# Last stage of a convolution, attention and expert kernel: next image's divisions moved ahead of seven weighings, GpSimd's residual ahead of folds, router logits read in PSUM

## The reference, cut to what matters

```python
t = t + _L1_attn_ref(_ln_t(t), ...)          # softmax(q k) v + x, added to t
z = _ln_t(t)                                 # zero mean, unit variance per token
router_probs = softmax(z @ router_w + router_b)      # 8 experts
top_p, top_i = top_k(router_probs, 2)
top_p = top_p / sum(top_p)
expert_out = einsum('bnd,edc->bnec', z, expert_w) + expert_b
t = t + sum over the two chosen experts of top_p * expert_out
```

## Time and profile before

| what | value |
|---|---|
| time before, median of 3 runs | 2733.99 us (2731.76 to 2734.71) |
| the profiled execution's own time | 2732.48 us |
| its span in the profile | 2730.6 us |
| its mean granted clock of TensorE | 0.917 of full speed |
| PE busy | 2417.7 us (89%) |
| DVE busy | 2352.5 us (86%) |
| ACT busy | 1599.9 us (59%) |
| POOL busy | 394.4 us (14%) |

### The profile page before, as it was taken

How to read it: one execution, slowest core, us unless ns; L and a number is a source line. 1 busy time by engine, 2 the same in 40 slices (tenths; PEclk the granted TensorE clock), 3 DMA queues, 4 the chain that set the end, 5 groups by cost and what they waited for, 6 DMA issues and landing times. The chain is left out here.

```text
span 2730.6 us, 46984 instructions
## 1 busy us (share of the span) xinstructions
PE 2417.7 (89%) x18454; PEld 968.7 (35%) x18454; DVE 2352.5 (86%) x4150; ACT 1599.9 (59%) x2106; POOL 394.4 (14%) x456
## 2 busy tenths in 40 slices
PE   3878879269999999999999999999999998888886
PEld 1343334112222222222222222222222225767764
DVE  4577776599999999999999999999999973999997
ACT  1243343337777777777777777777777773333333
POOL 0011111300000001000000000000000001555555
PEclk9989999579999999999999999999999996766677
DMA  7686784420202212202202112022020002232321
GB/s 172 159 246 202 215 249 128 152 57 1 60 1 60 60 66 60 60 1 60 57 4 60 39 22 60 16 45 60 1 60 25 1 25 83 72 98 81 108 72 24
DMA packets 68110, 206.29 MB, mean 76 GB/s; under 512 B 20630, under 2 KB 33554, under 8 KB 61234
## 3 DMA queue, kind: packets, MB, share of 16 engines
q1 hardware_dynamic: 64034, 185.27, 24.3%
q0 software_dynamic: 3040, 15.57, 1.5%
q10 hardware_dynamic: 816, 2.46, 0.3%
HBM read 80.14 MB, written 61.31 MB: 52 GB/s over the span
## 5 line engine op out<-in xcount | busy, mean ns | idle before, releaser
L1331 DVE TENSOR_REDUCE at_XM<-at_psX 128x1 f32<-128x448 f32 x2688 | 1546.1, 619 | 88.6 <-PE at_psX L1182 67.9
L1248 ACT ACTIVATE at_PR<-at_psS 128x896 f32<-128x896 f32 x1344 | 1162.9, 915 | 451.2 <-PE at_psS L1158 449.1
L1200 PE MATMUL at_psV<-at_PR,at_V 128*32 128x448 f32 x5376 | 644.4, 551 | 0.1
L1158 PE MATMUL at_psS<-at_US,at_KS 128*128 128x448 f16 x2688 | 635.0, 356 | 0.6 <-ACT at_PR L1248 0.2
L1182 PE MATMUL at_psX<-at_KS,at_US 64*128 64x448 f16 x1344 | 489.7, 364 | 65.5 <-DVE at_XM L1331 43.0
L1182 PE MATMUL at_psX<-at_KS,at_UH 64*128 64x448 f16 x1344 | 489.7, 364 | 0.0
L1182 PEld LDWEIGHTS at_psX<-at_KS,at_US 64*128 64x128 f16 x1344 | 124.6, 93 | 720.0 <-DVE at_XM L1331 659.9
L1158 PEld LDWEIGHTS at_psS<-at_US,at_KS 128*128 128x128 f16 x2688 | 200.7, 98 | 272.7 <-ACT at_PR L1248 119.3
L1297 POOL CAST at_mrow<-at_mt 7x128 f16<-7x128 f32 x64 | 17.9, 279 | 1609.7 <-DVE at_mt L1350 1256.8
L1594 POOL TENSOR_TENSOR fi_WE<-fi_WE 128x256 f32<-128x256 f32 (+1 forms) x224 | 199.4, 922 | 197.0 <-DVE fi_WE L1647 197.0
L389 PE MATMUL psA<-sb_stacks,sb_lhs 128*32 128x448 f32 x1568 | 157.0, 547 | 0.8 <-DVE sb_X L841 0.8
(11 more groups left out here) (200 smaller groups left out, 2062.1 us busy)
## 6 DMA issues: line engine op xcount, KB each, us to landing
sums<-at_O SPq DMA_DIRECT2D x16, 1568.0 KB, 6.3
fi_SUMS<-sums SPq DMA_DIRECT2D x16, 1568.0 KB, 6.7
sb_stacks<-sb_T SPq DMA_DIRECT2D x64, 270.5 KB, 6.7
sb_stacks<-sb_Xp SPq DMA_DIRECT2D x64, 248.8 KB, 8.6
sb_stacks<-sb_Xp SPq DMA_DIRECT2D x64, 248.0 KB, 5.5
sb_stacks<-sb_T SPq DMA_DIRECT2D x64, 172.5 KB, 9.0
at_KS<-key_stacks SPq DMA_DIRECT2D x32, 208.0 KB, 6.8
fi_RES<-residual SPq DMA_DIRECT2D x16, 400.0 KB, 7.3
```

Source lines behind the costliest of these rows:

```text
L1158: last = nc.tensor.matmul(psS[:, at % 2, k, 0:TILE], KS[:, b, (2 * c + k) * P:(2 * c + k + 1) * P], US[:, b, t * TILE:(t + 1) * TILE], sta ...
L1200: last = nc.tensor.matmul(psV[C * q:C * q + C, 0:TILE], V[:, b, G * k + q, :], PR[:, (n * 2 * STEPS + 2 * q4 + q // 2) % PRS, q % 2, :], s ...
L1248: nc.scalar.activation(PR[:, f % PRS], psS[:, at % 2, :, 0:TILE], ACT.Exp).then_inc(p_ready, 1)
L1331: nc.vector.tensor_reduce(o, psX[:, (at + j) % 3, 0:TILE], AX.X, ALU.max).then_inc(x_done, 1)
```

## The change

In `finish`:

- VectorE does the inversions and divisions of image n + 1 directly behind L1696 and ahead of weighings 7 to 12.
- GpSimd does the residual of image n + 1 ahead of the folds that stand at s = 3 (the first fold of set 3, the second of set 2), and not behind all folds. In step 0, which has no folds, it stays where it was. Step 15 has no next image and so no residual.
- ScalarE's copy of the logits is gone. VectorE's L1707, L1708 and L1713 read them in PSUM; L1713 writes `LG` and gives `lg_ready`, for which TensorE's fifth set of sums waits.

```diff
@@ ScalarE
-                    act.wait_ge(l_full, n + 1)
-                    nc.scalar.activation(LG[:].rearrange("p k e -> p (k e)"), psL, ACT.Copy).then_inc(lg_ready, 1)
                     act.wait_ge(gap_ready, n + 1)
@@ GpSimd
+                nxt = n + 1 < N
                 if n > 0:
                     for s in range(QSETS + 1):
+                        if nxt and s == 3:
+                            residual(n + 1, (c + 1) % TURN, r + b)
                         if s < QSETS:
...
-                if n + 1 < N:
+                elif nxt:
                     residual(n + 1, (c + 1) % TURN, r + b)
@@ VectorE
                 nc.vector.tensor_copy(Z16[:, :, 3, :], Z16[:, :, 1, :]).then_inc(z16_ready, 1)
-                weigh(m, mb, range(7, NU))
                 if nxt:
                     invert(n + 1, 0)
                     invert(n + 1, 1)
                     settled()
                     for h in range(2):
                         divide(n + 1, (c + 1) % TURN, h)
-
-                dve.wait_ge(lg_ready, n + 1)
+                weigh(m, mb, range(7, NU))
+
+                dve.wait_ge(l_full, n + 1)
                 rev3 = rev[:].unsqueeze(1).broadcast_to([P, NC, E])
-                link(nc.vector.tensor_reduce(top1[:], LG[:], AX.X, ALU.max))
-                link(nc.vector.tensor_tensor(CAND[:], LG[:], per_token(top1[:], E), ALU.is_equal))
+                logits = psL.rearrange("p (k e) -> p k e", e=E)
+                link(nc.vector.tensor_reduce(top1[:], logits, AX.X, ALU.max))
+                link(nc.vector.tensor_tensor(CAND[:], logits, per_token(top1[:], E), ALU.is_equal))
...
-                link(nc.vector.scalar_tensor_tensor(out=LG[:], in0=SEL1[:], scalar=-3e38, in1=LG[:], op0=ALU.mult,
-                                                    op1=ALU.add))
+                nc.vector.scalar_tensor_tensor(out=LG[:], in0=SEL1[:], scalar=-3e38, in1=logits, op0=ALU.mult,
+                                               op1=ALU.add).then_inc(lg_ready, 1)
+                dve.wait_ge(lg_ready, n + 1)
```

## The result

| | before | after |
|---|---|---|
| median of 20 runs | 2733.35 us (2727.85 to 2738.29) | 2737.44 us (2730.19 to 2741.46) |
| profiled execution, its span | 2732.48, 2730.6 | 2734.93, 2733.1 |
| DVE busy | 2352.5 us | 2334.6 us |
| ACT busy | 1599.9 us | 1594.7 us |

The ratio is 1.0014, 95% interval 1.0007 to 1.0020: slower by 4 us, within the 0.2% that the forecast called no change. VectorE is busy for 18 us less, and the kernel is not faster.

What follows compares the result with a forecast made beforehand. VectorE bounds the kernel; its path changes by +0.75 + 0.01 - 1.73 + 0.45 = -0.52 us a step, but late clock rises hold steps at 27.3. +3.7 on 2734.0 gives 2737.7 us; case range 2733 to 2742, 8 in 10 2724.5 to 2745.

Steps and rivals of the forecast that it cites:

- The case it rested on: Last stage: short and long steps alternate with early and late clock rises, mean 27.3 us; chance 0.52.
- Part 1: Divisions ahead of weighings 7 to 12: TensorE's unit-9 experts and the work queued behind them come 1.11 us later.
- The break: Gap of 0.9 us in TensorE's burst after its first eight transposes, which can only delay the clock's rise.
- Part 2: Logits read in PSUM: L1707 begins 0.04 us behind the router; three reads cost 0.00 to 0.05 us a step.
- The Trainium skill's fixed cost: VectorE's three PSUM reads: 62 extra cycles each, 3.1 us in sum over 16 images; as a rival, chance 0.05.
- Part 3: Residual ahead of the folds: new stalls in VectorE's routing of 0.3 to 0.65 us a step, taken as 0.45.
- TensorE next: Experts of unit 2, slack 0.3 us: a late clock rise stalls VectorE's third weighing 1.2 to 1.8, taken as 1.45.
- The mean near 27.3: Steps of the last stage: mean length held at the spacing of the clock's rises, 27.3 us.
- the alternation that was drawn: Last stage: steps of about 26.5 and 28 us, short and long in turn.
- The ends: Step 0 gains 0.35 us, step 15 gains 0.45, where the alternation stands is worth up to 1; 0.7 taken off.
- the correction to the median: Profiled execution lay 1.5 us below the median, so +4.5 for it became +3.7 against the median of 2734.0.

Runs made afterwards that it cites:

- res_last: The changed kernel with GpSimd's residual put back behind all folds; 2736.70 us, ratio 1.0012 to the kernel before.
- fill: The changed kernel with eight transposes repeated in TensorE's wait for weighing 7; 2723.51 us, ratio 0.9965 to the kernel before.
- strewn: The changed kernel with inversions and divisions spread among weighings 7 to 12 and the residual two sets of folds later; 2717.35 us, ratio 0.9948 to before.
- psum_only: The kernel before with only the logits read in PSUM and ScalarE's copy gone; 2729.10 us, ratio 0.9982.

## Why the prediction was right

The forecast was +3.7 us on the median and the result +4.1. The case it rested on is the one that came: VectorE's saving is kept in steps with an early rise and taken back by a stall behind TensorE where the rise is late. That the number agrees within 0.4 us is in part luck, as the last three points say.

- **Part 1.** The break is 0.88 us (forecast 0.9), and the experts of unit 9 begin 1.91 us behind the first transpose where they began 0.83 behind it: 1.08 later, forecast 1.11.
- **Part 2.** Routing begins 0.04 behind the router, and the reads from PSUM cost 5 ns, nothing and nothing (groups of 16: 368, 367 and 362 ns long; from SBUF 363 for the reduce and 367 for L1713 of the kernel before). The Trainium skill's fixed cost ("VectorE: DVE Perf Modes", The TRN2 errata), 3.1 us by the estimate, does not appear.
- **Part 3.** L1711 to L1721 lose 0.23 to 0.26, 0.01, 0.02 and 0 or 0.17: 0.3 to 0.45, forecast 0.45. A step without a stall is 26.44 to 26.46, forecast 26.5. The rule that an operation with both inputs in SBUF waits for GpSimd's running instruction, read from two rows, held in all ten kernels: each such operation of 200 elements that met one ended at least 0.22 us behind it, most of them 0.22 to 0.23, and those that read PSUM did not wait. The Trainium skill has it as a lock ("SBUF — State Buffer", Who interferes with whom).
- **TensorE next.** The stall ahead of the third weighing is 0.95 to 1.52 us in eight steps, 1.22 in the mean (forecast 1.2 to 1.8, taken as 1.45), long steps are 27.4 to 27.9 (forecast 27.95). Late rises come 2.8 to 3.6 us behind the experts, forecast 3.0 to 4.5.
- **The mean near 27.3, and the reason given for it.** From step 3 to step 13 it is 27.40. The pattern is one short step to two or three long ones, and not the alternation that was drawn; that came in `res_last`. The reason, that the rises keep a spacing of 27.3 and hold the steps to it, is too simple. The rises of the changed kernel lie at 2384.4, 2411.7, 2439.0 and 2462.9, so 27.3, 27.3 and 23.9 us apart, and the next one 30.7 later; in `res_last` they are 23.9 and 30.7 apart in turn; in `fill` 23.9 or 27.3, and the steps there have a mean of 26.28. The rises follow TensorE's bursts, in uneven jumps. What holds the mean is the exchange that the forecast also named: short steps bring a late rise, and its stall makes the next step long.
- **The ends.** The 14 steps are 2.2 us longer than before, not 6.0 less 0.7. The steps from 1, 2 and 13 are short (26.35, 26.44 and 26.46), and the largest miss is the last: 25.14 from step 14 to 15, where 27.3 had been put down. The forecast had seen that step 15 has no divisions, and missed that the delay and the break of part 1 are then gone as well. From step 0 to step 1 it had a gain of 0.35 for the copy; that interval is 0.53 longer (25.82 against 25.29), since part 1 already delays TensorE in step 1.
- **The reason for the correction to the median is not shown.** "That execution lay 1.5 below the median, I think because of where its rises fell": no run tells this, but the 20 runs of the kernel before spread over 10 us, and the last stage, whose first step is almost the same code in all of these kernels, reaches its first routing instruction at 2299.7 in one and at 2305.7 in another. What comes ahead of that point alone scatters by more than the term that was corrected. In the profiled executions the change is +2.45 us (2732.48 to 2734.93), where +4.5 was forecast for them; against the medians of 20 it is +4.1. So the close agreement of the number is not evidence for the terms at the ends.

```profile
2299.69 0.37 DVE L1714 TENSOR_REDUCE fi_top<-fi_psB 128x25 f32<-128x200 f32 x1 [3.69 <-PE fi_psB L1484]
```

```profile
2305.65 0.37 DVE L1706 TENSOR_REDUCE fi_top<-fi_psB 128x25 f32<-128x200 f32 x1 [3.70 <-PE fi_psB L1484]
```

(These are of `strewn` and of `psum_only`.) That scatter is why the mean step, read inside the last stage, tells more of a change of this size than one time does.

## What to carry to other kernels

An operation that is moved ahead of an engine's hand-over to TensorE costs the delay, and it can cost more through the break that it leaves in a burst of matmuls, behind which the clock may rise late. Look for the place where the bound engine waits for TensorE anyway and put the work there, a piece to a wait. Where the clock swings within each step of a loop, and TensorE has little slack at the low clock, a saving on the bound engine can vanish whole: before giving it up, close the break and measure it again.

## What the runs showed of the hardware

- Eight repeated transposes, work that nobody reads, made the kernel 14 us faster (2737.44 to 2723.51). With four of them three late rises were left, with none nine, in one profiled execution each.
- Steps of a program and rises of the clock can lock to each other: `res_last` ran for thirteen steps at 27.15 and 27.45 in turn, mean 27.29, with rises 23.9 and 30.7 apart in turn.
- The wait between VectorE and GpSimd goes both ways: the residual takes 1.88 us, and 2.00 where an operation of VectorE with both inputs in SBUF gets in at its start.
- The same wait costs VectorE about 1.75 us a step that this change did not touch. In all ten kernels the folds of sets 0 to 2 hold three operations of the norm, each of 25 elements, to 0.04 us behind their ends: 0.54, 1.13 and 0.65 us long in steps with folds, 0.18, 0.19 and 0.19 in step 0, which has none. One of them, L1684, has only one tensor as input, so two SBUF inputs are not the only form that waits. Here are two of them in step 5 of the changed kernel, and GpSimd's folds:

```profile
2422.26 0.54 DVE L1684 TENSOR_SCALAR fi_lvar<-fi_lvar 128x25 f32<-128x25 f32 x1
...
2423.64 1.13 DVE L81 TENSOR_TENSOR fi_ltmp<-fi_lrs 128x25 f32<-128x25 f32 x1
```

```profile
2420.81 1.95 POOL L1592 TENSOR_TENSOR fi_WE<-fi_WE 128x512 f32<-128x512 f32 x2 [2.89 <-DVE fi_WE L1648]
2423.47 1.95 POOL L1592 TENSOR_TENSOR fi_WE<-fi_WE 128x512 f32<-128x512 f32 x2 [0.71 <-DVE fi_WE L1648]
```
